# Moving the self term and the gate multiply of a selective scan out of the scan stage, with raw sums copied by ScalarE, a four-slot x^T ring, eight q slots and GpSimd multiplies in pairs

## The chip, the cores and the metric

One core of one Trainium2 chip runs the whole program in one launch. The metric is the time of the launch on the device in microseconds, lower is better. The profile has engines PE (TensorE; PEld is its weight load), DVE (VectorE), ACT (ScalarE), POOL (GpSimd) and SP (SyncE, which here only issues DMAs).

## What is computed

x has 2 x 4096 tokens of 512 columns. All arithmetic is fp32.

```python
xn = layernorm(layernorm(x)) * gamma + beta
x_ssm, z = split(xn @ W_in.T)                 # 1024 channels each
x_ssm = silu(causal_conv4(x_ssm) + conv_b)
xp = x_ssm @ W_xproj.T                        # 33 columns
B, C = xp[..., 1:17], xp[..., 17:33]
dt = softplus(xp @ W_dt.T + b_dt) + 0.001
# scan over time, 1024 channels x 16 states:
h = clip(exp(A*dt)*h + (1-exp(A*dt))/A * B * x_t, -10, 10)
y_t = sum_n(C_n * h_n) + D * x_t
x = x + (y * silu(z)) @ W_out.T
# mixture stage: shared product + one expert product scaled by the
# sum of the normalised top-2 gate weights
xf = layernorm(x)
out = x + xf @ W_shared.T + wsum * (xf @ W_expert.T) + bias
```

## The kernel before, in words

The program has four stages, one after another, each with its own block of instructions for every engine: `setup`, `front` (layer norm, input product, convolution, xp, dt; it writes x_ssm, silu(z), dt, a split transpose of x_ssm and B, C to DRAM), `scan`, and `ffn` (output product, residual, second layer norm, gates, shared and expert product). Every stage works on 16 chunks of 512 tokens. In `scan` a chunk has 8 blocks m of 128 channels, and a block has 16 steps, one for each state n. So there are 128 blocks and 2048 steps.

The scan keeps a transformed state. One step is spread over the engines:

- PE `make_d` (L896): a product of the transposed x (`xk`, two half-block slots) with a band matrix of B (`dm`, new for each chunk) gives one 512-column piece of d for the next block in one of two PSUM banks. ACT `move_d` (L847) copies it to `dd`.
- ACT `make_a` (L864): exp of dt times a constant, for the state three steps ahead, into one of four PSUM banks.
- DVE `states` (L1000): one scan instruction of 128x512 from `dd` and `ps_a` to one of 8 slots of `g`.
- POOL (L836): `q = g * C_n`, 128x512, in one of 4 slots of `q`. It waits for the scan and for the sum that frees the slot.
- PE `sum_state` (L917): a true fp32 product of q with a diagonal weight, added in `ps_y` over the 16 states, four steps (`LAG`) behind `make_d`.
- ACT `keep` (L871): every four steps, the last column of four g slots to `carry`.

Once a block there are four more operations. POOL multiplies B and C of the chunk (L815, once a chunk), PE weighs them (`weigh_bc`, L904, an fp32 product into a `ps_d` bank), DVE `self_term` (L961) makes `t = (ps_d + D) * x_ssm`, PE adds t to `ps_y` through the identity (L915), and DVE `finish` (L955) makes `y = ps_y * silu(z)` in the slot of z, which SP stores. DVE does `finish` after step 6 and `self_term` after step 7 of a block.

SP issues all loads of the scan from one queue in a written order with waits between them. For each block it loads dt, x_ssm, silu(z) (256 KB each), the diagonal weights (1.06 MB) and two halves of x^T (three pieces of 132 KB each). For each chunk it also loads `cc`, the spread C rows (four pieces of 1 MB), and `dm` (four pieces of three times 264 KB), both around the border between two chunks: `dm` in the block m = 6, `cc` in m = 7 and in m = 0 of the next chunk. Loads for the chunk after the last one wrap around to chunk 0, and so does the last block's `make_d`.

In `ffn`, PE does for each chunk 16 transposes (`L1241`), 96 matmuls of fp32r for the output product of the next chunk (four `project` calls), 12 for the gates, and 96 for the shared and expert products. fp32 operands are split in a high and a low part, with three matmuls for each pair of tiles. y is split by ACT (`y_hi`, L1167) and POOL (`y_lo`, L1145, 128x4096). POOL also adds the bias (L1159) and raises to the power -1/2 (L1140). The output product is made for one chunk ahead; in the last chunk it is made once more for chunk 0, and not used.

Of the kernel before, what the change touches and what calls it, by code (L numbers as in the profile page):

```python
# [4 lines left out]
P = 128  # L5
BATCH, LEN, DM = 2, 4096, 512
DI, NS, TAPS, NX = 1024, 16, 4, 33
TOKENS = BATCH * LEN
CH = 512
# [10 lines left out]
BLK = 32  # L20
# [23 lines left out]
def build(nc, t_in, out):  # L44
    with ExitStack() as ctx:
# [28 lines left out]
        scan(nc, sb, sem, ident, clips, xs_d, dt_d, zs_d, xp_d, xt_d, bt_d, band_d, c_d, w_d, y_d)  # L74
        ffn(nc, sb, sem, t_in, ident, minus_half, y_d, out)
# [524 lines left out]
def scan(nc, sb, sem, ident, clips, xs_d, dt_d, zs_d, xp_d, xt_d, bt_d, band_d, c_d, w_d, y_d):  # L600
    STEPS = MD * NS
    CHUNKS = BATCH * NCH
    AB, GB, QB = 4, 8, 4
    LEAD = 3
    LAG = 4
    HALF = NBLK // 2
    BC_AT, FINISH_AT, T_AT = 6, 6, 7
    PIECES = 4
    EACH = NBLK // PIECES
    with ExitStack() as c:  # L610
        w = sb("w_s", [P, 2, W_BIG], c=c)
        small = sb("small", [P, MD, W_SMALL], c=c)
        xs, dt = sb("xs_s", [P, 2, CH], c=c), sb("dt_s", [P, 2, CH], c=c)
        x_prev = sb("x_prev", [P, 2, 1], c=c)
        zs = sb("zs_s", [P, 2, CH], c=c)
        cc = sb("cc", [P, NS, CH], c=c)
        dm = sb("dm", [ROWS, NBLK, BLK, NS], F32R, c)
        xk = sb("xk", [ROWS, 2, HALF, P], F32R, c)
# [3 lines left out]
        t = sb("t", [P, CH], c=c)  # L622
        bc, c_r = sb("bc", [NS, CH], c=c), sb("c_r", [NS, CH], c=c)
        b_ahead = sb("b_ahead", [P, NS], c=c)

        neg_u0 = sb("neg_u0", [P, NS], c=c)
        fac, lim = sb("fac", [P, CH, 2], c=c), sb("lim", [P, CH, 2], c=c)
# [5 lines left out]
        s_pass, s_init = S("pass"), S("init")  # L633
        s_sm, s_band, s_bcl, s_ba = S("small"), S("band"), S("bcl"), S("ba")
        s_dm = [S(f"dm{i}") for i in range(PIECES)]
        s_xk, s_cc = [S("xk0"), S("xk1")], [S(f"cc{i}") for i in range(4)]
        s_dtl, s_wl, s_xsl, s_zsl = ([S(f"{n}{e}") for e in range(2)] for n in ("dt", "w", "xs", "zs"))
        s_bc, s_dps, s_dd, s_bcm, s_t = S("bc"), S("dps"), S("dd"), S("bcm"), S("t")
        s_a, s_g, s_q, s_n, s_fin = S("a"), S("g"), S("q"), S("n"), S("fin")
        s_car, s_zero, s_slow = S("carry"), S("zero"), S("slow")  # L640
        s_yo = [S("yo0"), S("yo1")]

        C_G, C_Q, C_N, C_FIN, C_T, C_CAR = AB, GB, LAG, 2, 1, 2

        def loads(ch, m):

            return ch * (16 * MD // 2) + 16 * (m // 2) + 16

        def scanned(ch, s):

            return ch * STEPS + s + C_G

        def multiplied(ch, s):

            return ch * STEPS + s + C_Q

        def summed(ch, s):

            return ch * STEPS + s + C_N

        with nc.Block() as block:
            @block.sync
            def _(sp):
                def load_x(b, k, m, h, n):
                    t0 = k * CH + (CH // 2) * h
                    for r, part in enumerate((0, 0, 1)):
                        src = xt_d[part, b, bass.ds(t0, BLK + 1), bass.ts(m, P)]
                        sp.dma_start(xk[(BLK + 1) * r:(BLK + 1) * (r + 1), h, :, :].bitcast(F32),
                                     bass.AP(tensor=src.tensor, offset=src.offset,
                                             ap=[(DI, BLK + 1), (BLK * DI, HALF), (1, P)])).then_inc(s_xk[h], 16)  # L670

                def fill_band(c, b, k):

                    for h in range(2):
                        sp.dma_start(band_d[c % 2, h, :, 0:2 * NS], bt_d[h, b, bass.ds(k * CH, CH + 1), :],
                                     allow_slow_non_contiguous=True).then_inc(s_band, 16)

                def load_b(c, i):
                    for r, part in enumerate((0, 1, 0)):
                        src = band_d[c % 2, part, bass.ds(BLK * EACH * i, BLK + 1), NS:2 * NS]  # L680
# [25 lines left out]
                def load_bc(b, k):  # L706
                    sp.dma_start(bc[:, :], xp_d[b, 1:1 + NS, bass.ds(k * CH + 1, CH)]).then_inc(s_bcl, 16)
# [668 lines left out]
```

## Time and profile before

| | us |
|---|---|
| median of 3 runs | 5179.3 (5155.68 to 5187.78) |
| the profiled execution's own time | 5171.58 |
| its span, first to last instruction | 5169.8 |
| scan, first to last DVE scan instruction | 1389.6 to about 4243 |
| first DMA of the last stage, its first matmul | 4259.66, 4285.25 |

| engine | busy share of the span |
|---|---|
| PE | 90% |
| DVE | 72% |
| ACT | 62% |
| POOL | 60% |

The shares are averages over stages with different limits. The granted TensorE clock is 0.94 of full speed in the mean. A busy time is a union of intervals: neighbouring instructions of an engine overlap by some tens of ns, so the spacing of instructions in a run of them is less than their mean duration.

### The profile page before, as it was taken

The page shows a single profiled execution, that of the slowest core. Times are in us where ns is not written, and L with a number is a line of the kernel's source. Part 1 is how long each engine was busy: PE and PEld are TensorE (multiplying, and loading weights), DVE is VectorE, ACT ScalarE, POOL GpSimd, SP SyncE. Part 2 cuts the span into 40 slices and gives each one's busy share as a digit, 9 for nine tenths or more (in the row PEclk, how much of TensorE's full clock was granted, in tenths as well). Part 3 has the DMA queues.
Part 4 walks back from the last instruction along what each step waited for, and adds up shares of the span by engine and source line. Part 5 has one row for each costly group of instructions (what it writes and reads, how often), then busy time and mean ns, then how long its engine had stood idle before and what let it go on. Part 6 is the DMA issues. An engine that isn't in the chain of part 4 may idle for free. (4 is left out here: it accounts for less than half of the span.)

```text
span 5169.8 us, 55997 instructions
## 1 busy us (share of the span) xinstructions
PE 4673.5 (90%) x14838; PEld 2749.7 (53%) x14838; DVE 3721.2 (72%) x4169; ACT 3205.7 (62%) x5723; POOL 3082.2 (60%) x2296
## 2 busy tenths in 40 slices
PE   4999999999598899989999989998899987999999
PEld 3566666666244444444444444444444446777777
DVE  5566666666498899889889988998898883333332
ACT  2545545545487788778888877887788772212111
POOL 1112122122298899889888988998898883322322
PEclk9889889889799999999999999999999998999999
DMA  4444444444656665665566566656655653222221
GB/s 176 145 153 163 158 150 164 161 146 165 190 163 177 190 171 170 181 190 169 170 185 185 163 179 182 174 163 191 182 172 165 191 170 130 81 81 81 81 72 66
DMA packets 590424, 807.29 MB, mean 156 GB/s; under 512 B 129738, under 2 KB 334866, under 8 KB 563735
## 3 DMA queue, kind: packets, MB, share of 16 engines
q1 hardware_dynamic: 544919, 721.30, 47.2%
q10 hardware_dynamic: 45312, 83.90, 4.3%
q8 instruction: 61, 1.00, 0.1%
q14 instruction: 132, 1.08, 0.1%
HBM read 561.72 MB, written 245.57 MB: 156 GB/s over the span
## 5 line engine op out<-in xcount | busy, mean ns | idle before, releaser
L836 POOL TENSOR_TENSOR q<-g,cc 128x512 f32<-128x512 f32 x2048 | 2535.9, 1277 | 329.8 <-PE ps_y L917 256.1
L1000 DVE TENSOR_TENSOR_SCAN g<-dd,carry,ps_a 128x512 f32<-128x512 f32 x2048 | 2444.4, 1257 | 256.6 <-ACT ps_a L864 140.7
L917 PE MATMUL ps_y<-q,w_s 128*128 128x512 f32 x4104 | 2186.6, 614 | 32.1 <-POOL q L836 32.1
L896 PE MATMUL ps_d<-dm,xk 99*128 99x512 f32 x2064 | 1650.9, 801 | 196.5 <-DMA xk<-xt_d 130.9
L847 ACT ACTIVATE dd<-ps_d 128x512 f32<-128x512 f32 x2064 | 1250.0, 606 | 550.2 <-PE ps_d L896 547.8
L864 ACT ACTIVATE ps_a<-dt_s,small 128x512 f32<-128x512 f32 x2051 | 1450.3, 707 | 0.0
L917 PEld LDWEIGHTS ps_y<-q,w_s 128*128 128x128 f32 x4104 | 794.0, 197 | 699.6 <-issue 405.2
L896 PEld LDWEIGHTS ps_d<-dm,xk 99*128 99x128 f32 x2064 | 403.3, 196 | 796.5 <-issue 653.4
L303 POOL TENSOR_TENSOR xnt_lo<-xnt_f,xnt_hi 128x512 fp32r<-128x512 f32 x68 | 92.3, 1359 | 622.0 <-ACT xnt_hi L329 619.6
L435 PE MATMUL ps_r_f<-xnt_hi,w_hi 128*128 128x512 f32 x1024 | 411.1, 401 | 12.1 <-ACT xz L345 7.5
L435 PE MATMUL ps_r_f<-xnt_hi,w_lo 128*128 128x512 f32 x1024 | 406.7, 397 | 0.0
L435 PE MATMUL ps_r_f<-xnt_lo,w_hi 128*128 128x512 f32 x1024 | 405.9, 396 | 0.0
L549 DVE SCALAR_TENSOR_TENSOR conv<-xz,taps,conv 128x512 f32<-128x512 f32 x384 | 352.0, 917 | 13.6
L1140 POOL TENSOR_TENSOR rstd_c<-var_c,minus_half 128x4 f32<-128x4 f32 x17 | 17.3, 1018 | 511.6 <-DVE var_c L1291 511.6
L315 POOL TENSOR_TENSOR lg_f<-lg_f,v_f 128x2048 f32<-128x2048 f32 x32 | 149.2, 4683 | 220.9 <-ACT lg_f L383 220.9
L1212 PE MATMUL ps_c<-wo_hi,y_hi 128*128 128x512 f32 x544 | 222.5, 409 | 40.4 <-DVE wo_lo L1299 37.8
L1283 DVE TENSOR_TENSOR x_c<-ps_c,x_c 128x512 f32<-128x512 f32 x68 | 47.0, 692 | 291.5 <-PE ps_c L1212 291.5
L435 PEld LDWEIGHTS ps_r_f<-xnt_hi,w_hi 128*128 128x128 f32 x1024 | 197.6, 193 | 58.4 <-ACT xz L345 11.1
L435 PEld LDWEIGHTS ps_r_f<-xnt_lo,w_hi 128*128 128x128 f32 x1024 | 197.2, 193 | 42.4
L435 PEld LDWEIGHTS ps_r_f<-xnt_hi,w_lo 128*128 128x128 f32 x1024 | 198.0, 193 | 40.5
L1212 PE MATMUL ps_c<-wo_lo,y_hi 128*128 128x512 f32 x544 | 218.5, 402 | 0.0
L1212 PE MATMUL ps_c<-wo_hi,y_lo 128*128 128x512 f32 x544 | 217.7, 400 | 0.0
(155 smaller groups left out, 4685.5 us busy)
## 6 DMA issues: line engine op xcount, KB each, us to landing
w_s<-w_d SPq DMA_DIRECT2D x129, 1088.0 KB, 5.1
xk<-xt_d SPq DMA_DIRECT2D x777, 132.0 KB
cc<-c_d SPq DMA_DIRECT2D x66, 1024.0 KB, 14.4
xt_d<-xt_f SPq DMA_DIRECT2D x256, 256.0 KB, 2.3
dm<-band_d SPq DMA_DIRECT2D x204, 264.0 KB
y_lo<-y_d SPq DMA_DIRECT2D x18, 2048.0 KB, 9.2
dt_s<-dt_d SPq DMA_DIRECT2D x129, 256.0 KB, 4.3
xs_s<-xs_d SPq DMA_DIRECT2D x129, 256.0 KB, 3.7
```

What stands on the lines that cost most here:

```text
L303: pool.tensor_tensor(xnt_lo[:, q, :], xnt[:, q, :], xnt_hi[:, q, :].bitcast(F32), ALU.subtract)\
L315: pool.tensor_tensor(lg[:, m0:m1, :], lg[:, m0:m1, :], v[:, m0:m1, :], ALU.add)\
L435: last = pe.matmul(ps_r[:, r % RING, :], wp[:, q, cols], xp_[:, q, :], start=(q + j == 0), stop=(q == KD - 1 and j == 2))
L549: dve.scalar_tensor_tensor(acc, xz[:, m, j:j + CH], taps[:, m, j:j + 1], acc, ALU.mult, ALU.add).then_inc(s_cv, 1)
L836: pool.tensor_tensor(q[:, s % QB, :], g[:, s % GB, :], cc[:, n, :], ALU.mult).then_inc(s_q, 1)
L847: act.activation(dd[:, m % 2, :, BLK * i:BLK * i + BLK], ps_d[:, ring(i), :].rearrange("p (t n) -> p n t", n=NS) if m == 0 else ps_d[:, (m ...
L864: act.activation(ps_a[:, s % AB, :], dt[:, m % 2, :], ACT.Exp, scale=small[:, m % MD, S_A + n:S_A + n + 1]).then_inc(s_a, 1)
L896: pe.matmul(ps_d[:, parity, :], xk[:, i // HALF, i % HALF, :], dm[:, i, :, :].rearrange("p t n -> p (t n)"), start=True, stop=True).then_i ...
L917: pe.matmul(ps_y[:, m % 2, :], w[:, m % 2, n * P:(n + 1) * P], q[:, s % QB, :], start=(n == 0), stop=(n == NS - 1)).then_inc(s_n, 1)
L1000: dve.tensor_tensor_scan(g[:, s % GB, :], dd[:, m % 2, n, :], ps_a[:, s % AB, :], carry[:, m, n:n + 1], ALU.add, ALU.mult).then_inc(s_g, 1)
L1212: last = pe.matmul(dst, a(j), b(j), start=(j + p == 0), stop=(j == tiles - 1 and p == 2))
L1283: dve.tensor_tensor(x[:, e, i, :], ps[:, i, :], x[:, e, i, :], ALU.add).then_inc(s_x1, 1)
```

## The change

In the scan stage the self term, the z load, the final multiply on DVE and its x_ssm load are gone. ACT copies the raw sum to a buffer `y` after step 10 of a block (`finish`), and that is what SP stores. POOL multiplies two steps at a time over 8 q slots, and the sums run six steps behind `make_d` instead of four. The x^T ring has four half-block slots, loaded up to a block further ahead. The pieces 2 and 3 of `cc` are issued at the end of m = 7 and the start of m = 0, and nothing is loaded or made past the last chunk. A path for clipping (not taken with these inputs) works in halves, to make room in SBUF.

In `ffn` the self term, the addition and the multiply by silu(z) are written out for every block of every chunk, for two chunks ahead. PE gets eight `weigh` products (48 rows, fp32r) per chunk, DVE eight `self_term` instructions, POOL sixteen 128x512 instructions (`mix`) and three for B * C (`weigh_rows`), SP eight loads each of x_ssm (ring of four) and silu(z) (ring of two). For chunk 0 DVE does the `mix`. `y_lo` is made in four parts. One half of a `project` is put between the second and the third transpose group, and the output product past the last chunk is left out. The weights are loaded from ACT's queue.

```diff
 def scan(...):
-    AB, GB, QB = 4, 8, 4
+    AB, GB, QB = 4, 8, 8
-    LAG = 4
+    LAG = 6
+    XB = 4
+    FINISH_AT = 10
 # SP
-                            load_x(*at(m + 1), 1, 0)
-                            load_dt_xs(*at(m + 1))
+                    load_x(blk + 2, 1)
+                    load_dt(blk + 1)
...
-                            load_x(*at(m + 2), 0, 0)
-                            load_zs(*at(m + 1))
+                    load_x(blk + 3, 0)
...
+                    if m == MD - 1 and more:
+                        sp.wait_ge(s_q, multiplied(NS * blk + 12))
+                        load_c(ch + 1, 2)
 # POOL
-                        pool.wait_ge(s_g, scanned(ch, s + 1))
-                        pool.wait_ge(s_n, summed(ch, s - QB + 1))
-                        pool.tensor_tensor(q[:, s % QB, :], g[:, s % GB, :], cc[:, n, :], ALU.mult).then_inc(s_q, 1)
+                    pool.wait_ge(s_g, s + 2)
+                    if s >= QB:
+                        pool.wait_ge(s_n, s - QB + 2)
+                    pool.tensor_tensor(q[:, s % QB:s % QB + 2, :], g[:, s % GB:s % GB + 2, :], cc[:, n:n + 2, :],
+                                       ALU.mult).then_inc(s_q, 2)
 # ACT
+                def finish(blk):
+                    act.wait_ge(s_n, NS * (blk + 1))
+                    if blk >= 2:
+                        act.wait_ge(s_yo[blk % 2], 16 * (blk // 2))
+                    act.activation(y[:, blk % 2, :], ps_y[:, blk % 2, :], ACT.Copy).then_inc(s_fin, 1)
 # PE: weigh_bc and the product with ident gone
 # DVE: finish and self_term gone
 def ffn(...):
 # SP, ring of two z tiles
+                def load_zs(ch, m):
+                        if piece(ch, m) >= ZRING:
+                            sp.wait_ge(s_mul, piece(ch, m) - ZRING + 1)
 # POOL, in each chunk
-                        rest_of_y(ch + 2, e, it * 16 + 32)
+                    mix(ch + 2)
+                    inverse_spread(ch + 1)
+                    rest_of_y(ch + 2)
+                    weigh_rows(ch + 3)
+                def mix(ch):
+                        for m in range(MD):
+                            pool.wait_ge(s_tt, piece(ch, m) + 1)
+                            pool.tensor_tensor(y[:, m, :], y[:, m, :], xs[:, m % XRING, :], ALU.add).then_inc(s_add, 1)
+                            pool.wait_ge(s_zsl[m % ZRING], 16 * (ch * (MD // ZRING) + m // ZRING + 1))
+                            pool.tensor_tensor(y[:, m, :], y[:, m, :], zs[:, m % ZRING, :], ALU.mult).then_inc(s_mul, 1)
 # DVE
+                def self_term(ch, m):
+                        dve.scalar_tensor_tensor(xs[:, m % XRING, :], ps_b[:, :], d_par[:, m:m + 1], xs[:, m % XRING, :],
+                                                 ALU.add, ALU.mult).then_inc(s_tt, 1)
 # PE, in each chunk
+                    turn(ch, 0)
+                    turn(ch, 1)
+                    project(ch + 1, 0, 0)
+                    turn(ch, 2)
+                    turn(ch, 3)
+                    weigh(ch + 2, 0)
+                    project(ch + 1, 0, 1)
```

## Rows read from the trace of the kernel before

**Rows 1.** Busy time by engine in two stretches: the scan, the last stage.

```profile
core 0: us, PE busy (x) PEld busy (x) DVE busy (x) ACT busy (x) POOL busy (x), PEclk, DMA share, GB/s
1399.00:4243.00 2844.00, 2633.64 (x6655) 1265.64 (x6654) 2582.39 (x2302) 2335.64 (x4605) 2552.50 (x2062) 0.96 0.62 177
...
4285.00:5170.00 885.00, 835.15 (x3680) 674.84 (x3680) 275.08 (x642) 160.37 (x181) 251.80 (x98) 0.97 0.23 78
```

**Rows 2.** Timeline of DVE in an undisturbed block (start, length, what).

```profile
2006.67 0.72 DVE L961 SCALAR_TENSOR_TENSOR t<-ps_d,small,xs_s 128x512 f32<-128x512 f32 x1
2007.32 17.67 DVE L1000 TENSOR_TENSOR_SCAN g<-dd,carry,ps_a 128x512 f32<-128x512 f32 x15
2024.90 0.66 DVE L955 TENSOR_TENSOR zs_s<-ps_y,zs_s 128x512 f32<-128x512 f32 x1
2025.49 1.27 DVE L1000 TENSOR_TENSOR_SCAN g<-dd,carry,ps_a 128x512 f32<-128x512 f32 x1
2026.67 0.72 DVE L961 SCALAR_TENSOR_TENSOR t<-ps_d,small,xs_s 128x512 f32<-128x512 f32 x1
```

**Rows 3.** Timeline of POOL, the undisturbed blocks of one chunk and one earlier run.

```profile
1999.03 9.87 POOL L836 TENSOR_TENSOR q<-g,cc 128x512 f32<-128x512 f32 x8
...
1966.95 121.92 POOL L836 TENSOR_TENSOR q<-g,cc 128x512 f32<-128x512 f32 x98 [0.80 <-PE ps_y L917]
```

**Rows 4.** Timeline of ACT and PE in undisturbed steps.

```profile
2003.07 0.59 ACT L847 ACTIVATE dd<-ps_d 128x512 f32<-128x512 f32 x1
2003.55 0.69 ACT L864 ACTIVATE ps_a<-dt_s,small 128x512 f32<-128x512 f32 x1
2004.16 0.20 ACT L871 ACTIVATE carry<-g 128x4 f32<-128x4 f32 x1
2004.26 0.59 ACT L847 ACTIVATE dd<-ps_d 128x512 f32<-128x512 f32 x1
...
2002.22 0.80 PE L896 MATMUL ps_d<-dm,xk 99*128 99x512 f32 x1
2003.31 0.80 PE L896 MATMUL ps_d<-dm,xk 99*128 99x512 f32 x1
```

**Rows 5.** Busy time, one whole chunk of the scan, and its border stretch.

```profile
1744.90:1922.60 177.70, 162.99 (x417) 78.43 (x416) 161.38 (x145) 145.93 (x290) 159.71 (x130) 0.97 0.63 178
1888.00:1966.00 78.00, 65.31 (x159) 30.84 (x158) 63.67 (x58) 56.12 (x110) 62.42 (x51) 0.93 0.84 218
```

**Rows 6.** Who waited for whom in the scan (total, times, longest).

```profile
PE ps_d L896 <- DMA xk<-xt_d: 120.8, 34, 6.6
DVE g L1000 <- ACT dd L847: 98.9, 45, 7.3
POOL q L836 <- DMA cc<-c_d: 61.9, 17, 5.8
```

**Rows 7.** Groups of POOL instructions of three widths (busy, mean ns).

```profile
L836 POOL TENSOR_TENSOR q<-g,cc 128x512 f32<-128x512 f32 x2048 | 2535.9, 1277 | 329.8 <-PE ps_y L917 256.1 <-DMA cc<-c_d 61.9 <-issue 0.5
L1145 POOL TENSOR_TENSOR y_lo<-y_lo,y_hi 128x4096 fp32r<-128x4096 f32 x18 | 162.8, 9044 | 20.8 <-ACT y_hi L1167 20.8
L315 POOL TENSOR_TENSOR lg_f<-lg_f,v_f 128x2048 f32<-128x2048 f32 x32 | 149.2, 4683 | 220.9 <-ACT lg_f L383 220.9
```

**Rows 8.** Last stage: chain by pieces, and PE's idle time at the transposes.

```profile
4378.17 11.72 PE ps_c L1212 x48
4389.89 2.80 PE ps_g L1212 x12
...
4799.67 12.54 PE ps_c L1212 x48
...
5135.89 28.10 PE ps_c L1212 x120
```

**Rows 9.** Timeline where the last stage starts.

```profile
4248.19 5.65 SPq L716 DMA_DIRECT2D y_d<-zs_s  x1
4259.66 0.38 SPq L1100 DMA_DIRECT2D o_c<-in_W_outT  x1
...
4267.05 2.29 DVE L1299 TENSOR_TENSOR wo_lo<-o_c,wo_hi 128x2048 fp32r<-128x2048 f32 x1 [18.89 <-ACT wo_hi L1171]
...
4274.19 8.85 POOL L1145 TENSOR_TENSOR y_lo<-y_lo,y_hi 128x4096 fp32r<-128x4096 f32 x1 [13.64 <-ACT y_hi L1167]
...
4275.95 9.25 DVE L1299 TENSOR_TENSOR wo_lo<-o_c,wo_hi 128x2048 fp32r<-128x2048 f32 x1 [6.60 <-ACT wo_hi L1171]
```

**Rows 10.** Timeline of PE in the last stage, with its idle time.

```profile
4641.15 1.09 PE L1241 MATMUL ps_t_c<-ident,xn_c 128*128 128x128 f32 x8 [2.51 <-DVE t_lo L1310]
```

**Rows 11.** DMA issues (count, KB each, us to landing).

```profile
zs_s<-zs_d SPq DMA_DIRECT2D x129, 256.0 KB, 3.8
bc<-xp_d SPq DMA_DIRECT2D x17, 32.0 KB, 14.6
```

More of the change, by code:

```diff
@@ L873, in _ @@
                 for i in range(NBLK):
[L874 removed]
+                    move_d(0, i)
                 act.wait_ge(s_sm, 16)
                 for s in range(LEAD):
[L877 to L886 removed]
+                    make_a(s)
@@ new lines, in rest_of_y @@
+                def rest_of_y(ch):
+                    if ch < CHUNKS:
+                        pool.wait_ge(s_yh, ch + 1)
+                        for j in range(YL):
+                            part = slice(2 * j, 2 * j + 2)
+                            pool.tensor_tensor(y_lo[:, part, :], y[:, part, :], y_hi[:, part, :].bitcast(F32), ALU.subtract)\
+                                .then_inc(s_yl, 1)
+                pool.memset(gate[:, :, :], -1.0).then_inc(s_set, 1)
+                pool.memset(raw_g, 0.0).then_inc(s_set, 1)
@@ new lines, in upper_y, with normalize @@
+                def upper_y(ch):
+                    if ch < CHUNKS:
+                        act.wait_ge(s_mul, piece(ch + 1, 0))
+                        if ch > 0:
+                            act.wait_ge(s_o, ch * SUB)
+                        act.activation(y_hi[:, :, :], y[:, :, :], ACT.Copy).then_inc(s_yh, 1)
+                def normalize(ch):
+                    if ch < CHUNKS:
+                        act.wait_ge(s_sh, ch + 1)
+                        for i in range(SUB):
+                            act.activation(xn[:, i, :], x[:, ch % 2, i, :], ACT.Identity, scale=rstd[:, i:i + 1],
+                                           bias=shift[:, i:i + 1]).then_inc(s_xn, 1)
@@ new lines, in store @@
+                def store(ch):
+                    act.wait_ge(s_fin, ch * SUB + SUB)
+                    act.dma_start(rows(out, ch), o[:, ch % 2, :, :]).then_inc(s_out[ch % 2], 16)
+                load_weights(1, "W_outT", 0)
+                load_weights(2, "W_outT", HALF * P)
+                load_weights(3, "W_sharedT", 0)
+                load_weights(4, "W_expertT", 0)
+                for i in range(3):
+                    upper_weights(i)
+                upper_y(0)
+                for i in range(3, len(parts)):
+                    upper_weights(i)
@@ L1220, in turn_gates @@
                     last.then_inc(s_g, 1)
-                def project(e, i):
-                    at = slice(i * P, (i + 1) * P)
-                    product(ps[:, i, :], lambda m: y_hi[:, m, at], lambda m: y_lo[:, e, m, at],
-                            lambda m: wo_hi[:, m, :], lambda m: wo_lo[:, m, :], MD).then_inc(s_o, 1)
-                pe.wait_ge(s_lo, 2)
-                pe.wait_ge(s_yl, 1)
+                pe.wait_ge(s_lo, 1)
+                for m in range(MD):
+                    weigh(0, m)
@@ L1270, in _, with step @@
                 at = [0]
-                def step(ins, base, wait=True):
+                def step(ins, wait=True):
                     at[0] += 1
```

951 lines of the change are left out of this document (481 added, 470 removed).

## The prediction

> **What bounds the kernel now.** I read busy time by stretch first, because the page's shares mix stages. In the scan's 2844 us DVE, PE and POOL are each busy for 90 to 93% of the time; in the last stage PE is for 94% and nothing else for over a third [rows 1]. So the scan is near a joint limit and the last stage is PE's. The front isn't touched.
>
> Next the timelines of an undisturbed block. DVE has no gap in it: 15 scans take 2024.90 - 2007.32 = 17.58 us, 1.172 each, one scan more takes 1.18, the self term holds DVE for 0.65 (2006.67 to 2007.32) and the final multiply for 0.59. Block after block that is 20.00 us (2006.67 to 2026.67) [rows 2]. POOL is as full: eight multiplies in a run begin 1.228 apart ((9.87 - 1.28) / 7), and 98 of them go without a gap worth a row [rows 3]. ACT needs 0.48 for a copy and 0.61 for an exp, 1.09 a step, and 0.10 more for a carry; PE's step is 1.09 too [rows 4].
>
> Last the borders. A chunk takes 177.7 us where eight blocks would be 160.0, so 17.7 us are lost per chunk [rows 5]. In the 78 us around a border DMA moves 218 GB/s with a busy share of 0.84, against 178 GB/s for the chunk, and the waits name the culprits: PE for `xk` 120.8 us in 34 waits, POOL for `cc` 61.9 in 17, DVE for `dd`, which is PE's stall handed on [rows 5, 6].
>
> **The change part by part.** The sum is made against the profiled execution's own 5171.6 us, 8 us under the median.
>
> *Undisturbed block.* DVE loses 0.65 + 0.59: 20.00 - 1.24 = 18.76 us. POOL would stay at 16 x 1.228 = 19.65 with single multiplies, so the pair's price decides. No row has a width of 1024. Between 1277 ns (512) and 4683 ns (2048) the line gives 1277 + 3406/3 = 2412 ns, towards 9044 ns (4096) it gives 2387 [rows 7]; less the 0.05 by which neighbours overlap, a pair holds POOL for 2.34 to 2.36 us, 18.7 to 18.9 a block. ACT has 16 x 1.09 + 4 x 0.10 and the new copy, 0.48 to 0.6: 18.4. PE has 16 x 1.09 = 17.4 [rows 4]. The largest is POOL's, so I take 18.9. Bounds are 18.76 (DVE alone) and 19.65 (a pair costs two singles). Gain: 128 x 1.1 = **141 us**, bounds 45 and 159. The wait for two scans puts POOL one step later; `LAG` 6 and eight q slots give the two steps back on the side of the sum, and g has eight slots, so I cost it at nothing. If that cover were gone each pair would wait for a PE step, which is the fourth rival's kind of loss.
>
> *Borders.* The two-slot x^T ring asks for a half within half a block, some 10 us, just when SP's queue is full. With four slots the load goes out a block or more ahead, past the 7.3 us of the longest wait. The last two `cc` pieces are asked for as soon as their slots are free, and per block 0.5 MB of x_ssm and silu(z) and 64 KB of weights are no longer loaded: 2.9 to 2.35 MB. Against a full cure: `dm` (3.2 MB) and `cc` (4.2 MB) still fall into about 52 us, with 2.75 x 2.35 = 6.5 MB beside them, 13.9 MB. At the 218 GB/s of [rows 5] that is 64 us, so a backlog of some 12 us builds up. `cc` and `dm` pieces have 12 to 15 us between slot free and use, and x^T over 20. So most is covered, not all. I take 5 us left of 17.7, bounds 0 and 17.7. Gain: 16 x 12.7 = **203 us**, bounds 0 and 283.
>
> *Ends of the scan.* The last store's issue waits 5.65 us in a queue full of loads for a chunk that isn't there, and 11.5 us pass until the next stage's first DMA [rows 9]. Those loads go: **-7**, bounds 0 and -10.
>
> *Start of the last stage.* First matmul 25.6 us after the first DMA now. The new chain: B and C rows land, three POOL instructions (3.8), `weigh`, then for eight blocks on DVE self term 0.7 and two operations of about 0.7 each. Silu(z) sits in a ring of two with a landing of 3.8 us [rows 11], issued behind the x, gate and bias loads, so I have the last block mixed at 38 us; `y_hi` 3.6 and `y_lo` 9.1 after it make 51. For chunk 1 POOL mixes before it serves the layer norm of chunk 0: another 4. **+31**, bounds +10 and +60.
>
> *PE's loop.* Eight `weigh` at the 2.80 / 12 = 0.233 us of a matmul [rows 8] are 1.9 us a chunk; the half `project` between the transposes covers the 2.5 us that PE waits there for `t_lo` [rows 10]. **-0.6 x 15 = -9**, bounds -20 and +30 with imperfect cover. DVE (five and a half us more) and POOL (below) have room beside 52.7 us a chunk, (4799.67 - 4378.17) / 8 [rows 8].
>
> *Last chunk.* 96 matmuls of a product that nobody reads are left out, 22.4 us on PE's path; 3 us of waits come out from under it. **-19**, bounds -15 and -22.
>
> Sum: -141 - 203 - 7 + 31 - 9 - 19 = **-348**, 5171.6 - 348 = 4824 us.
>
> One rule is weighed against a row. While POOL made `y_lo` from 4274.19 to 4283.04, a DVE subtract that takes 2.29 us took 9.25 and ended 2.2 us after POOL [rows 9]. The change puts POOL's `mix` beside three DVE instructions a chunk with both inputs in SBUF (the gate scaling, `pick`, `shift`). I count them at nothing, since PE has the 22 us of the shared and expert products to do and needs DVE's first sum only 11 us into them. The Trainium skill (SBUF — State Buffer, Who interferes with whom) says that a VectorE instruction with two SBUF inputs and a GpSimd instruction that reads SBUF block each other for a whole instruction; by that rule, the trace agrees. It also says that one with at most one SBUF input doesn't, which fits the scans running at full rate beside POOL [rows 2, 3]; what it would cost is the third rival.
>
> **The rivals.** (1) *The borders stay.* DMA volume, not ring depth, is the limit, and 12 us or more of the 17.7 remain. For: 218 GB/s and the backlog above. Against: most waits are for `xk` [rows 6]. Price at 16 us left: 16 x 11 = +176, 5000 us.
> (2) *A pair costs two singles.* POOL then sets 19.65 us a block: 128 x 0.75 = +96, 4920 us. That is also the case in which the change doesn't do what it says; the wide rows speak against it [rows 7].
> (3) *`mix` on POOL delays the gates* by a POOL instruction of 1.28 us for each of three or four DVE instructions, and the cover isn't there: 16 x 5 = +80, 4905 us.
> (4) *Slower than before.* POOL's loop in the last stage is 4 x 1.29 + 16 x 1.23 + 1.0 + 9.1 + 3.8 = 38.8 us. Silu(z) has two slots, so three turns of the ring take 3 x (landing + 1.6) in place of 3 x 4.9. With 3.8 us of landing nothing is lost. But small loads in a full queue landed after 14.6 us [rows 11]: the loop is then 72.7 us and the gain is down to 28. From 15.4 us on the whole gain is gone; at 18 us it is 83 us, 16 x 30 = +480, 5305 us. Against: DMA in the last stage carries 78 GB/s now [rows 1] and 4 MB more per chunk make it some 156, under the scan's 178 [rows 5].
> (5) *Nothing is left at the borders*: -80, 4745 us.
>
> **How the numbers follow.** Chances: forecast 0.50, (1) 0.13, (2) 0.12, (3) 0.08, (4) 0.05, (5) 0.12. The range 4730 to 4960 takes in the forecast with its bounds for the start, (2), (3) and (5); (1) and (4) lie above it. A change of 1% is about what a measurement of this kernel can tell. Faster by over 1%: 0.94; within 1%: 0.02 (the mild form of (4)); slower: 0.04.
>
> **What the changed profile would show.** Undisturbed blocks of 18.9 us with POOL gapless and DVE with small gaps; POOL pairs of about 2.41 us; hardly any wait of PE for `xk`; chunks of about 156 us. In the last stage chunks of about 52 us, no 2.5 us gap at the transposes, first matmul some 50 us after its first DMA. Wrong would be: pairs of 2.5 us, DVE or PE waiting over 10 us at each border, or PE in the last stage waiting for POOL's power or for `y_lo`.

## The result and the profile after

The changed kernel takes 4989.4 us (median of 4 runs, 4966.86 to 5004.33), 0.963 of the time before (95% interval 0.957 to 0.968). The forecast was 4825 with a range of 4730 to 4960: the sign was right, the size was not, 3.7% gained against 6.8%. The profiled execution took 4966.86 us. I cut it where the kernel does, at the first and last scan instruction and the first DMA of the last stage:

| stretch | before | after | change | forecast |
|---|---|---|---|---|
| start to first scan | 1389.6 | 1381.0 | -9 | 0 |
| first to last scan | 2852.3 | 2611.5 | -241 | -344 |
| last scan to first DMA of last stage | 17.7 | 7.6 | -10 | -7 |
| last stage | 910.1 | 965.0 | +55 | +3 |

The first line is scatter: other kernels with this front unchanged start their scan between 1366 and 1407 us. Almost the whole miss lies in the two large lines.

DVE's timeline over one chunk of the scan (start, length, what, idle before and its releaser), with the first and the last scans of all:

```profile
1380.98 3.62 DVE L927 TENSOR_TENSOR_SCAN g<-dd,carry,ps_a 128x512 f32<-128x512 f32 x3 [20.17 <-ACT ps_a L811]
...
1577.84 18.93 DVE L927 TENSOR_TENSOR_SCAN g<-dd,carry,ps_a 128x512 f32<-128x512 f32 x16 [10.84 <-ACT dd L800]
1598.22 131.30 DVE L927 TENSOR_TENSOR_SCAN g<-dd,carry,ps_a 128x512 f32<-128x512 f32 x112 [1.45 <-ACT dd L800]
1741.36 58.81 DVE L927 TENSOR_TENSOR_SCAN g<-dd,carry,ps_a 128x512 f32<-128x512 f32 x50 [11.83 <-ACT dd L800]
...
3899.84 92.62 DVE L927 TENSOR_TENSOR_SCAN g<-dd,carry,ps_a 128x512 f32<-128x512 f32 x79
```

Away from the borders DVE has no gap: 131.30 / 7 = 18.757 us a block, where it was 20.00 [rows 2]. At the border it still has gaps of 10.84 and 1.45 us. The chunk takes 1741.36 - 1577.84 = 163.5 us against 8 x 18.76 = 150.1, so 13.5 us are lost where 17.7 were [rows 5].

Over the whole scan that splits without a choice of chunk. I call what exceeds 128 undisturbed blocks the rest (borders and both ends): before 2852.3 - 128 x 20.00 = 292, after 2611.5 - 128 x 18.757 = 211. So blocks gave 159 us and the rest 82. The table of the experiments uses the same rest.

POOL in its longest run, with the page's group for it:

```profile
1600.81 112.47 POOL L789 TENSOR_TENSOR q<-g,cc 128x1024 f32<-128x1024 f32 x48 [1.53 <-DVE g L927]
```
```profile
L789 POOL TENSOR_TENSOR q<-g,cc 128x1024 f32<-128x1024 f32 x1024 | 2398.5, 2365 | 252.6 <-DVE g L927 93.8
```

A pair occupies POOL for 112.47 / 48 = 2.343 us, 18.75 a block, the lower end of the forecast's 2.34 to 2.36.

Who waited in the scan (total, times, longest):

```profile
DVE g L927 <- ACT dd L800: 189.3, 26, 15.2
ACT ps_a L811 <- DMA dt_s<-dt_d: 156.2, 16, 13.6
...
POOL q L789 <- DMA cc<-c_d: 39.6, 13, 4.2
```

PE no longer waits for `xk` at the borders (120.8 us in all in [rows 6]; one wait of 5.1 us is left, at the start). ACT waits for `dt_s` instead, once per border, 13.6 us at most where `xk` had 6.6. SP's own timeline at that border says why:

```profile
1703.94 5.98 SPq L691 DMA_DIRECT2D cc<-c_d  x1
1709.96 0.65 SPq L698 DMA_DIRECT2D b_ahead<-xp_d  x1
1710.66 10.43 SPq L700 DMA_DIRECT2D x_prev<-xs_d  x1
1721.13 1.75 SPq L706 DMA_DIRECT2D y_d<-y  x1
1722.92 0.55 SPq L691 DMA_DIRECT2D cc<-c_d  x1
1723.52 1.85 SPq L660 DMA_DIRECT2D xk<-xt_d  x3
1725.41 0.54 SPq L691 DMA_DIRECT2D cc<-c_d  x1
1725.99 0.59 SPq L683 DMA_DIRECT2D dt_s<-dt_d  x1
```

A 4 KB DMA keeps SP for 10.43 us. `dt_s`, due for the next block, is issued at 1725.99 behind it and behind two 1 MB pieces of `cc`, and ACT goes on at 1738.93 after 10.47 us of waiting. The load that is held stands directly behind `b_ahead`, 16 values of B for each of 128 partitions, 2048 single elements of 4 bytes in 8 KB. The same was so in the kernel before, where the three `xk` loads behind it held SP for 9.12 us:

```profile
1925.45 0.44 SPq L712 DMA_DIRECT2D b_ahead<-xp_d  x1
1925.93 9.12 SPq L668 DMA_DIRECT2D xk<-xt_d  x3
```

The last stage, in the chain that ended last (start, length):

```profile
4006.61 17.34 DMA y_c<-y_d
...
4048.13 14.34 POOL y_lo L1143 x4
4062.60 8.28 PE ps_c L1235 x24
...
4110.62 9.27 POOL y_lo L1143 x4
4119.93 5.49 PE ps_c L1235 x12
...
4151.30 24.79 PE ps_c L1235 x108
...
4205.30 24.79 PE ps_c L1235 x108
```

The first matmul of the output product comes 4062.6 - 4000.1 = 62.5 us after the stage's first DMA (25.6 before, [rows 9] and the table of times): +37. (The `weigh` products come before it, from 4017.59.) The product of chunk 1 starts 57.3 us later (37.4 before): +20. A chunk takes 54.0 us against 52.7 [rows 8]: 15 x 1.3 = +20. The unread product is gone: -21. Sum +56, of the +55 seen.

### The profile page after: what moved, and what is told of

Read it like the earlier page. It is cut to its first block and busy times, and to the rows that moved or that the text cites. A ratio compares the mean times of both kernels' runs of the same rounds, so it can differ in the third digit from the quotient of the medians.

```text
span 4965.1 us, 51915 instructions
## 1 busy us (share of the span) xinstructions
PE 4489.3 (90%) x14330; PEld 2559.1 (52%) x14330; DVE 3653.8 (74%) x4044; ACT 3221.7 (65%) x5827; POOL 3270.8 (66%) x1585
## 5 line engine op out<-in xcount | busy, mean ns | idle before, releaser
L927 DVE TENSOR_TENSOR_SCAN g<-dd,carry,ps_a 128x512 f32<-128x512 f32 x2048 | 2407.4, 1255 | 223.8 <-ACT dd L800 189.3
L789 POOL TENSOR_TENSOR q<-g,cc 128x1024 f32<-128x1024 f32 x1024 | 2398.5, 2365 | 252.6 <-DVE g L927 93.8
L867 PE MATMUL ps_y<-q,w_s 128*128 128x512 f32 x4096 | 2161.8, 609 | 122.0 <-POOL q L789 122.0
L811 ACT ACTIVATE ps_a<-dt_s,small 128x512 f32<-128x512 f32 x2048 | 1512.6, 739 | 161.6 <-DMA dt_s<-dt_d 156.2
L800 ACT ACTIVATE dd<-ps_d 128x512 f32<-128x512 f32 x2048 | 1299.1, 635 | 110.7 <-PE ps_d L856 94.5
L856 PE MATMUL ps_d<-dm,xk 99*128 99x512 f32 x2048 | 1205.6, 590 | 106.6 <-ACT dd L800 66.5
L435 PE MATMUL ps_r_f<-xnt_hi,w_hi 128*128 128x512 f32 x1024 | 410.4, 401 | 13.4 <-ACT xz L345 9.0
L549 DVE SCALAR_TENSOR_TENSOR conv<-xz,taps,conv 128x512 f32<-128x512 f32 x384 | 352.1, 917 | 13.6
L1132 POOL TENSOR_TENSOR y_c<-y_c,xs_c 128x512 f32<-128x512 f32 x120 | 154.5, 1288 | 164.2 <-DVE xs_c L1353 164.2
L504 DVE TENSOR_TENSOR xt_f<-ps_t_f,xt_f 128x512 fp32r<-128x512 f32 x128 | 88.1, 688 | 176.2 <-ACT xt_f L324 176.2
L1235 PE MATMUL ps_c<-wo_hi,y_lo 128*128 128x512 f32 x512 | 205.7, 402 | 0.0
L1235 PE MATMUL ps_c<-wo_lo,y_hi 128*128 128x512 f32 x512 | 205.1, 401 | 0.0
## 6 DMA issues: line engine op xcount, KB each, us to landing
cc<-c_d SPq DMA_DIRECT2D x64, 1024.0 KB, 14.9
```

Of the source, the lines that this page charges most:

```text
L435: last = pe.matmul(ps_r[:, r % RING, :], wp[:, q, cols], xp_[:, q, :], start=(q + j == 0), stop=(q == KD - 1 and j == 2))
L549: dve.scalar_tensor_tensor(acc, xz[:, m, j:j + CH], taps[:, m, j:j + 1], acc, ALU.mult, ALU.add).then_inc(s_cv, 1)
L789: pool.tensor_tensor(q[:, s % QB:s % QB + 2, :], g[:, s % GB:s % GB + 2, :], cc[:, n:n + 2, :], ALU.mult).then_inc(s_q, 2)
L800: act.activation(dd[:, blk % 2, :, BLK * i:BLK * i + BLK], ps_d[:, i % 2, :].rearrange("p (t n) -> p n t", n=NS), ACT.Copy).then_inc(s_dd, 1)
L811: act.activation(ps_a[:, s % AB, :], dt[:, blk % 2, :], ACT.Exp, scale=small[:, blk % MD, S_A + n:S_A + n + 1]).then_inc(s_a, 1)
L856: pe.matmul(ps_d[:, i % 2, :], xk[:, (2 * blk + i // HALF) % XB, i % HALF, :], dm[:, i, :, :].rearrange("p t n -> p (t n)"), start=True, s ...
```

## The experiments

All times are medians; "rest" is the scan's span in the run's one profiled execution less 128 x 18.757 us, "C landing" the median time from issue to landing of a `cc` piece. The runs were made in five groups (e1 to e4, e5 to e8, e9 to e12, e13 to e16, e17 and e18), and the kernel before had medians of 5169.4 to 5189.2 us beside them. So between groups 20 us of a median mean little, and the ratios and rests are the better measure.

| run | us | ratio to before (95%) | rest | C landing |
|---|---|---|---|---|
| after | 4989.4 | 0.963 (0.957 to 0.968) | 211 | 14.9 |
| e1_prev_spread | 4994.8 | 0.962 (0.956 to 0.967) | 220 | 15.8 |
| e2_dt_first | 4959.5 | 0.957 (0.952 to 0.962) | 189 | 14.8 |
| e3_no_cc_reload | 4797.2 | 0.926 (0.921 to 0.931) | 15 | not reloaded |
| e4_single_multiply | 5014.7 | 0.970 (0.963 to 0.977) | 234 | 13.2 |
| e5_two_xk_slots | 5009.2 | 0.967 (0.958 to 0.975) | 227 | 12.9 |
| e6_no_dm_reload | 4893.5 | 0.943 (0.935 to 0.950) | 122 | 10.4 |
| e7_weigh_128_rows | 4946.9 | 0.953 (0.945 to 0.961) | 214 | 14.9 |
| e8_weigh_twice | 4995.2 | 0.964 (0.957 to 0.972) | 213 | 15.0 |
| e9_cc_ring_of_five | 4906.8 | 0.949 (0.945 to 0.954) | 129 | 15.1 |
| e10_cc_from_distinct_rows | 4865.4 | 0.943 (0.938 to 0.947) | 95 | 10.3 |
| e11_before_no_cc_reload | 4984.0 | 0.966 (0.962 to 0.971) | 92* | not reloaded |
| e12_ring_pad_early | 4864.8 | 0.942 (0.938 to 0.946) | 125 | 14.3 |
| e13_copies_32 | 4869.5 | 0.938 (0.933 to 0.942) | 100 | 10.4 |
| e14_copies_128 | 5144.1 | 0.991 (0.988 to 0.994) | 102 | 11.3 |
| e15_best_128_copies | 5051.4 | 0.974 (0.969 to 0.979) | 53 | 10.3 |
| e16_no_ring_128_copies | 5072.7 | 0.978 (0.973 to 0.983) | 73 | 10.2 |
| e17_best_32_copies | 4760.7 | 0.919 (0.916 to 0.922) | 51 | 10.5 |
| e18_no_ring_32_copies | 4782.8 | 0.921 (0.917 to 0.925) | 69 | 10.2 |

\* against 128 x 20.00, the blocks of before, whose own rest is 292.

**e1: `x_prev` in eight small DMAs, one per block.** Is the held SP the fault of that DMA's 4-byte pieces?

```diff
-                    sp.dma_start(x_prev[:, :], xs_d[b, :, :, bass.ds(k * CH, 1)].rearrange("m p o -> p (m o)"), ...)
+                    if m > 0 and more:
+                        load_prev(ch + 1, m - 1)        # 128 elements each
```

> The changed kernel with x_prev (1024 elements of 4 bytes, one DMA at the chunk border) loaded in eight DMAs of 128 elements, one in each block. Theory A (that DMA holds SP's queue for 10 us at the border, so that dt for the next block goes out late): the wait of ACT for dt falls from 156 us in all to under 50, a border costs 13.5 - 10 = 3 to 5 us, the time falls by 16 x 9 = about 145, to 4845. Theory B (the volume of dm and cc at the border is the limit): SP is held by the next DMA instead, a border keeps over 10 us, the time falls by less than 40.

No gain. SP at the same place of the border:

```profile
1735.90 0.99 SPq L698 DMA_DIRECT2D b_ahead<-xp_d  x1
1736.93 10.09 SPq L703 DMA_DIRECT2D x_prev<-xs_d  x1
```

An eighth of the pieces is held for as long, while the median of all 128 small loads is 0.43 us: the time isn't the load's own, and the name in the row is that of a victim. What stands in front of it is the same at all 15 borders: `b_ahead`. The load behind it is held for 10.1 to 12.0 us here, 10.4 to 11.9 in the kernel after, 8.2 to 9.6 (three `xk` loads) in the kernel before, 6.5 to 8.3 in e13, where C is read faster, and 4.6 to 7.7 in e3, where it isn't reloaded; elsewhere in the scan of the kernel after, its start and end aside, no load or store holds SP for over 7 us. So C has a part in it, and `b_ahead`'s single elements may have another. Only the path for clipping uses `b_ahead` and `x_prev`, so they could have been left out; no run does that.

**e2: dt ahead of a chunk's last `cc` piece in SP's order.** `x_prev` stays ahead of both.

```diff
                     load_x(blk + 2, 1)
+                    sp.wait_ge(s_a, NS * blk + 1)
+                    load_dt(blk + 1)
                     if m == 0:
...
                         load_c(ch, 3)
-                    sp.wait_ge(s_a, NS * blk + 1)
-                    load_dt(blk + 1)
```

> The changed kernel with the load of dt in a chunk's first block put ahead of the last cc piece. Theory A: x_prev's DMA still holds SP ahead of both, dt gains one cc piece of transfer at most, 16 x 4 = 64 us or less. Theory B: dt jumps one of the queued megabytes, 4 us a border, 64 us. Theory C (only the written order of dt behind cc is at fault): the wait for dt goes, 16 x 9 = 145 us.

The median falls by 30 us, the rest by 22, half of the 64 that theories A and B allow and far from theory C's 145. ACT's wait is down, and others grow in its place:

```profile
PE ps_y L867 <- POOL q L789: 155.0, 65, 12.8
DVE g L927 <- ACT dd L800: 139.5, 29, 15.2
ACT dd L800 <- PE ps_d L856: 99.2, 71, 9.3
ACT ps_a L811 <- DMA dt_s<-dt_d: 90.2, 19, 8.3
```

The order decides who is late, not whether somebody is.

**e3: C is loaded for the first chunk only. e6: the same for `dm`.**

```diff
                 def load_c(ch, i):
+                    if ch > 0:
+                        return
```

All later chunks then multiply by the first chunk's C, or in e6 use its B.

> The changed kernel with cc loaded for the first chunk alone, so that all later chunks multiply by the first chunk's C (that part of the computation is changed). 4.2 MB less at each border, x_prev's DMA kept. Theory B: the border's loss goes, 16 x 13 = about 200 us. Theory A: the DMA of small pieces still takes as long to issue, but dt no longer queues behind 2 MB; half of the loss may stay, 60 to 110 us gained.

> The changed kernel with dm (the band of B) loaded for the first chunk alone, so that later chunks use the first chunk's B (that part of the computation is changed). 3.2 MB less at each border, cc kept. Volume theory: the deficit of 2.8 MB (12 us at 218 GB/s) goes: -150 to -200 us, as without cc. If it is something of the cc loads themselves (their slow packets, or POOL's wait on them): less than -80 us.

Without the reload of C 192 us go, and with them the borders. The busy times of 1200 us in the middle of that scan (length, PE, PEld, DVE, ACT, POOL, clock, DMA share, GB/s):

```profile
2000.00:3200.00 1200.00, 1185.23 (x3072) 516.00 (x3071) 1199.34 (x1025) 1184.32 (x2368) 1199.10 (x512) 1.00 0.50 150
```

DVE misses 0.7 us of 1200. Without the reload of `dm` 96 us go, between the two expectations. Both are far more than the waits for these loads: `cc` has 39.6 us there, `dm` 4.3. The sum of bytes doesn't hold in full either: without `dm`'s 3.2 MB the backlog of the prediction's sum (12 us at 218 GB/s, 2.6 MB) would be gone, and still over half of the rest stays (122 of 211).

**e4: one step per multiply. e5: two x^T slots.** The two parts of the change that the forecast valued most, each undone.

```diff
-                for s in range(0, BLOCKS * NS, 2):      # e4
+                for s in range(BLOCKS * NS):
...
-    XB = 4                                              # e5, loads one block later
+    XB = 2
```

> The changed kernel with POOL multiplying one step at a time, still with eight q slots and the sums six steps behind. If POOL's time per step sets the block, blocks go from 18.75 to 19.65 us, +115 us less what the borders' waits absorb, 80 to 115. If DVE's scan sets it with room to spare on POOL, no change.

> The changed kernel with two half-block slots for x^T, as before the change, each loaded when its slot is free. Volume theory (what a border loses is DMA bytes over rate; the depth of the x^T ring matters little): 0 to +25 us. Depth theory of the prediction (most of the border's loss in the kernel before was the two-slot ring): +100 us or more, with PE waiting for xk as before, 100 us or more in all.

Pairs are worth 25 us, where 80 to 115 were expected, four slots 20; each is at the edge of what the intervals resolve. POOL in e4:

```profile
2068.40 152.72 POOL L789 TENSOR_TENSOR q<-g,cc 128x512 f32<-128x512 f32 x124 [2.00 <-DMA cc<-c_d]
```

Singles take 152.72 / 124 = 1.232 us, 157.7 for a chunk's 128. The borders make a chunk last 164 anyway, and DVE's blocks beside it still take 18.8 us: POOL falls behind inside the buffers and catches up at the border. While borders cost 13 us, a dearer multiply hides in them. In e5 PE waits 187.4 us for `xk`, more than before the change, and it costs 20.

**e7: `weigh` on 128 rows, the lower 80 zero. e8: each 48-row `weigh` twice.**

```diff
-        inv = sb("inv_c", [ROWS3, MD, P], F32R, c)
+        inv = sb("inv_c", [P, MD, P], F32R, c)        # e7, b_r alike
...
+                        pe.matmul(ps_b[:, :], inv[:, m, :], b_r[:, :], start=True, stop=True)   # e8
                         pe.matmul(ps_b[:, :], inv[:, m, :], b_r[:, :], start=True, stop=True).then_inc(s_bcm, 1)
```

> The changed kernel with the operands of weigh padded with zeros from 48 to 128 rows. In the trace a weigh adds 0.63 us to PE, 0.40 more than a matmul of 128 rows. If the change of row count between neighbouring matmuls costs that: 112 weighs in the loop x 0.40 = -45 us. If it comes from the change of weights, operands or PSUM bank: no change.

> The changed kernel with every weigh product done twice in a row. If the switch into and out of 48 rows costs, the second one costs a plain 0.23 us: +30 us. If each matmul of 48 rows costs 0.63: +75 us.

A `weigh` among its neighbours in the kernel after, then in e8 (start, busy time of one):

```profile
4305.30 0.40 PE L1235 MATMUL ps_c<-wo_hi,y_lo 128*128 128x512 f32 x1
4305.63 0.50 PE L1245 MATMUL ps_b<-b_r,inv_c 48*128 48x512 f32 x1
4306.06 0.50 PE L1235 MATMUL ps_c<-wo_hi,y_hi 128*128 128x512 f32 x1
4306.39 0.39 PE L1235 MATMUL ps_c<-wo_lo,y_hi 128*128 128x512 f32 x1
```
```profile
4302.54 0.39 PE L1235 MATMUL ps_g<-t_hi,wg_lo 128*128 128x512 f32 x1
4302.86 0.49 PE L1245 MATMUL ps_b<-b_r,inv_c 48*128 48x512 f32 x1
4303.19 0.39 PE L1246 MATMUL ps_b<-b_r,inv_c 48*128 48x512 f32 x1
4303.52 0.50 PE L1235 MATMUL ps_c<-wo_hi,y_hi 128*128 128x512 f32 x1
4303.85 0.39 PE L1235 MATMUL ps_c<-wo_lo,y_hi 128*128 128x512 f32 x1
```

From 4305.30 to 4306.39 three steps take 1.09 us; two matmuls of 128 rows would take 0.46, so the `weigh` adds 0.63. With two of them it is 4302.54 to 4303.85, 1.31 us, so the second adds 0.22 or 0.23 and a 48-row matmul itself costs what a wide one does (the loop grows from 54.0 to 55.8 us, 8 x 0.23; the median, 6 us up, doesn't resolve that). The other 0.40 is the change of row count, there and back. On 128 rows it is gone:

```profile
4172.57 24.59 PE ps_c L1239 x108
4223.64 24.58 PE ps_c L1239 x108
```

The spacing over the loop is 51.05 us per chunk, 15 x 2.95 = 44 us less; the median says 42.

**e9: a ring of five C pieces, with dt first.** If C is the cost, a piece asked for four blocks ahead should hide it. SBUF for the fifth comes from three x^T slots and six q slots.

```diff
-        cc = sb("cc", [P, NS, CH], c=c)
+        cc = sb("cc", [P, NS + 4, CH], c=c)
...
+                    at = 4 * ((4 * ch + i) % 5)
...
+                    if m == 3 and more:
+                        sp.wait_ge(s_q, multiplied(NS * MD * ch))
+                        load_c(ch + 1, 0)
```

> The changed kernel with a ring of five cc pieces, so that one of the four megabytes per chunk is loaded in the quiet block m = 3; to make room q has six slots (sums five steps behind) and x^T three, and dt is loaded ahead of cc as in the run with dt first. Volume theory: 1.05 MB less at a border is 5 us at 218 GB/s, 75 us over 15 borders beyond the 30 of dt first: about -105 against the changed kernel, if the smaller rings cost nothing. If order or ring depth rules: the smaller rings cost more than this gives, 0 or slower.

-83 us where 105 were expected, 53 of it beyond e2 (60 by the rest). The other three pieces still fall at the border.

**e10: as many bytes to `cc`, but each partition reads a row of its own (of dt).** In the kernel C lies in 16 copies, and eight partitions read each.

```diff
-                    src = c_d[:, ch // NCH, ch % NCH, 4 * i * CH:(4 * i + 4) * CH]
+                    src = dt_d[ch // NCH, (ch + i) % MD, :, (i % 2) * 4 * CH:(i % 2) * 4 * CH + 4 * CH]
```

> The changed kernel with cc loaded with the same bytes, packets of 8 KB and places in the queue, but from rows of dt that are distinct for each partition (that part of the computation is changed), where the kernel reads each row of C for eight partitions. cc's packets take 550 ns for 8 KB, those of w 392 to 467 for 8.7 KB. If reading one row eight times is what makes them slow: packets of 400 to 450 ns, the border's loss falls by a third to a half, -60 to -100 us. If the bytes alone count: no change.

124 us less by the medians, 116 by the rest, at the same volume, and a piece lands in 10.3 us, not 14.9. So at one volume it matters much how the rows are read; e6 shows that the volume counts too.

**e11: the kernel before, C loaded once.** Was that so already?

> The kernel before with cc loaded for the first chunk alone. Volume theory: its 17.7 us a border was mostly queueing behind bytes too, so nearly all goes, -200 to -270 us. Depth theory of the prediction (the two-slot x^T ring is the cause): PE still waits for xk, less than half goes, under -130 us.

Yes: the time falls by 185 us (5169.4 for the kernel before beside it), the rest from 292 to 92. So 200 us of the old borders hung on C, where the waits had 61.9 for `cc` and 120.8 for `xk` [rows 6].

**e12: e9, e7 and the weight parts split ahead of the first `mix`.**

```diff
-                for i in range(3):
+                for i in range(5):
                     upper_weights(i)
                 upper_y(0)
```

> The ring of five cc pieces with dt first, weigh padded to 128 rows, and the low parts of the weights made on DVE before the first chunk's mix, where DVE waits for y (in the changed kernel they share time with POOL's y_lo, which takes 14.3 us there in place of 9.3). Sum of the parts: -105 - 42 - 6, to about 4835.

-42 against e9, which e7 explains alone; the sum of the parts, 4835, is missed by 30 us. The early weights do what they should, but it is little: `y_lo` takes 9.69 us at the start and ends 65.5 us after the last scan, not 14.34 and 70.0.

**e13 and e14: 32 and 128 copies of C, so four partitions and one read a row.** e10 changed the place of the rows too; these change only the sharing (and the size of the front's store of C), and compute the right thing.

```diff
-COPIES = 16
+COPIES = 32     # e14: 128
```

> The kernel after with 32 copies of C in DRAM in place of 16, so that each row of C is read by four partitions in place of eight. The scan's loads keep their number and size; the front writes 0.5 MB more per chunk. Theory A (reads of one row by many partitions are slow, and that is most of what the distinct rows gained: -124 us): a part of that gain comes with each halving; with two halvings left after this one I expect 30 to 60 us less than the kernel after, 4930 to 4960, and cc landing after 12 to 14 us. Theory B (not the sharing; the distinct rows gained because they came from other places of DRAM, or because their bytes were just read by others): no change, 4980 to 5000, landing 14.9.

> The kernel after with 128 copies of C, one for each partition: no row is read twice, as with the distinct rows, but the product is the right one. The front writes 3.5 MB more per chunk in a store of its own, at 218 GB/s some 16 us of DMA beside 80 us of work; the front has DMA to spare, so 0 to +10 us in all, if the store doesn't delay the next ones in its queue. Theory A: scan span falls by about 130 to 150 us as with the distinct rows (4865), landing about 10.3 us, in all 4860 to 4900. Theory B: scan unchanged, 4990 to 5020 in all. If the front pays more than 50 us for the store, theory A can be right in the scan and the total still 4920.

One number makes the kernel 120 us faster. Both have about the rest of e10 (100 and 102, with 95 there) with C's own tensor, so sharing is the cause and the place of dt's rows isn't. I expected the gain to come in steps and the time with 32 copies to be 4930 to 4960; all of it comes between eight readers and four. The 36 us up to the first scan behind a border, in the kernel after, in e13 and in e6 (columns as above):

```profile
1705.00:1741.00 36.00, 25.54 (x61) 10.94 (x60) 24.53 (x21) 23.67 (x48) 24.68 (x12) 0.89 0.91 207
```
```profile
1710.00:1746.00 36.00, 30.34 (x74) 13.20 (x73) 29.46 (x26) 28.46 (x58) 29.89 (x14) 0.92 0.86 255
```
```profile
1708.00:1744.00 36.00, 30.86 (x76) 13.13 (x75) 30.20 (x27) 29.40 (x60) 30.62 (x14) 0.95 0.92 216
```

The DMA engines are nearly as busy and move 255 GB/s, not 207. e6, with eight readers and no `dm`, still moves only 216 at a share of 0.92. Neighbouring borders say the same: 202 to 212 in the kernel after, 243 to 266 in e13. The landing is the weaker sign. It falls from 14.9 to 10.4 us in e13, but it is 10.4 in e6 with eight readers too, and 12.9 to 15.8 in the other runs with 16 copies: it counts what stands in the queue as well.

128 copies lose it all in the front, where I had allowed 10 us: its store is 4 MB per chunk and stands in SP's queue ahead of the others. The scan starts at 1669 us, not 1381, DVE waits there 410.4 us for `x_f` (67.7 in the kernel after), and the read of x lands after 11.7 us, not 6.5.

**e15 to e18: is the late C one cause or two?** e12's version and the same without the longer ring (dt first, `weigh` on 128 rows and early weights stay), with 128 and with 32 copies.

> The version with the five-piece ring of C, the 128-row weigh, the early weight parts and dt first (4864.8), with 128 copies of C. Theory A: packets and ring both shorten the same waits, so the gains don't add: borders of 8.7 us are left of which half goes, 40 to 90 us less, 4775 to 4825. Theory B: 4865 or more.

> As the last, but without the ring of five C pieces and with the four x^T slots and eight q slots of the kernel after. Theory A: the faster landing does by itself what the ring does; 4780 to 4840, within 30 us of the version with the ring. Theory B: no gain from copies, so only the parts -30 (dt first), -42 (weigh) and some -20 (early weights) remain: 4900.

> The version with the five-piece ring of C, the 128-row weigh, the early weight parts and dt first (4864.8), with 32 copies of C, which cost the front nothing that the run with 32 copies shows apart (its scan started at 1405 us, that of other runs with an unchanged front between 1366 and 1407). With 128 copies the scan of this version fell by some 60 us against 16 copies; theory A: 32 copies do the same, 4790 to 4820. Theory B (the ring already hides what the slow reads cost): within 15 us of 4865.

> The same without the ring of five C pieces, with four x^T slots and eight q slots as in the kernel after. Theory A (one cause, late C pieces, cured twice): 5 to 25 us more than with the ring, as with 128 copies (5072.7 against 5051.4): 4800 to 4840. Theory B (two causes): 40 us or more above the version with the ring.

With dt first the rest is 189 (e2). The ring alone makes it 125 to 129, the copies alone 69, both 51: the gains of 60 to 64 and 120 don't add to 180 or more but give 138. That is what one cause would do, C pieces that come late: a faster read cures most of it and a longer lead a part of what is left. e15 and e16 missed their numbers by e14's front (5144.1 - 4869.5 = 275 us); less that they lie at 4777 and 4798, inside them. e17 and e18 came out below theirs, and differ by 22 us, inside the 5 to 25 of one cause. e17 is the fastest kernel here, 4760.7 us, 0.919 of before. Its scan, and what waits are left:

```profile
2016.61 18.85 DVE L929 TENSOR_TENSOR_SCAN g<-dd,carry,ps_a 128x512 f32<-128x512 f32 x16 [2.93 <-ACT dd L802]
2035.64 131.31 DVE L929 TENSOR_TENSOR_SCAN g<-dd,carry,ps_a 128x512 f32<-128x512 f32 x112 [0.18 <-ACT dd L802]
2168.99 150.04 DVE L929 TENSOR_TENSOR_SCAN g<-dd,carry,ps_a 128x512 f32<-128x512 f32 x128 [2.03 <-ACT dd L802]
```
```profile
DVE g L929 <- ACT dd L802: 47.4, 25, 6.9
ACT ps_a L813 <- DMA dt_s<-dt_d: 44.5, 14, 5.9
```

A chunk is 2168.99 - 2016.61 = 152.4 us, 2.3 above eight blocks.

## Why the prediction was right or wrong

- **Undisturbed block: right.** 18.9 us forecast, 18.76 measured; 141 against 159 us. DVE and POOL are within 0.01 us of each other, so the line through other widths (2.34 to 2.36) sized the pair well. But the rival "a pair costs two singles", priced at +96, was priced without the borders' waits, in which a slower POOL catches up; with those that stayed, e4 cost 25.
- **Borders: the step that failed.** "So most is covered, not all. I take 5 us left of 17.7." 13.5 were left; the rest fell by 82 us, not by the 210 of border and end terms. Two things were wrong. The cause was read off the wait with the largest total, `xk`. e5 and e11 show that it wasn't: with two slots PE waits for `xk` again and 20 us are lost, and without C's reload 200 of 292 us go even in the old kernel. `xk` was the small load that stood behind `cc` and `b_ahead` in one queue; the change took it out of the way, and `dt_s` took its place. And the backlog of 12 us, which the step worked out itself, was let off against the "12 to 15 us between slot free and use" of single pieces. But the pieces share one queue with all that is due sooner, so a backlog of 12 us delays those too. Taken at its word that sum leaves 12 us a border, 4825 + 16 x 7 = 4937 us; 13.5 were measured. That nearness is in part luck: the sum makes bytes at one rate the whole of it, and e6 and e13 show that it isn't (without `dm` no backlog is left in the sum, but 1743.99 - 1587.96 - 8 x 18.757 = 6.0 us are lost at the border in e6's trace; with four readers the bytes are the same and 111 us of the rest go). The case stood as the first rival, with 16 us and 5000, at a chance of 0.13.
- **The first rival was right in size and half right in reason.** It blamed the volume. The same volume from rows with four readers costs 110 us less of scan (e13) and moves at 255 GB/s, so 207 GB/s was the rate of this way of reading. The forecast used [rows 5]'s 218 GB/s as if it were a property of the DMA. Less volume helps as well (96 us in e6).
- **Ends of the scan: right**, -7 against -10.
- **Start of the last stage: too small**, +31 against +57. The `mix` of chunk 0 was done 44.3 us after the first DMA, not 38. `y_lo` was set at 9.1 and took 14.33, since DVE's weight splits run beside it (in e12, where they come earlier, it takes 9.69):

```profile
4044.32 4.49 DVE L1339 TENSOR_TENSOR wo_lo<-o_c,wo_hi 128x2048 fp32r<-128x2048 f32 x2
4048.13 14.33 POOL L1143 TENSOR_TENSOR y_lo<-y_c,y_hi 128x1024 fp32r<-128x1024 f32 x4 [30.68 <-ACT y_hi L1184]
4049.88 3.28 DVE L1339 TENSOR_TENSOR ws_lo<-xn_c,ws_hi 128x2048 fp32r<-128x2048 f32 x1 [1.08 <-ACT ws_hi L1176]
4053.09 4.42 DVE L1339 TENSOR_TENSOR we_lo<-xb_c,we_hi 128x2048 fp32r<-128x2048 f32 x1
4057.43 2.82 DVE L1339 TENSOR_TENSOR wg_lo<-x_c,wg_hi 128x512 fp32r<-128x512 f32 x1
```

 The last takes 2.82 us for a quarter of the elements that take 3.28, so it is mostly waiting. By the rule of the Trainium skill (SBUF — State Buffer, Who interferes with whom) cited in the prediction such DVE and POOL instructions take turns; the trace agrees, 14.33 us beside them and 9.27 for the same four at 4110.62. The prediction applied it to the loop and not to the start, where it costs 5 us on the path. Chunk 1's `mix`, priced at 4, and its `weigh` products amid the first output products, cost 20 together.
- **PE's loop: wrong sign**, -9 against +20, by one price: `weigh` at the 0.233 us of a 128-row matmul, where it costs 0.63. e7 makes it 0.23, and the loop is 51.05 us, 1.6 under before; the cover of the transposes was, if anything, better than the 0.6 forecast.
- **Last chunk: right**, -19 against -21.
- **The other rivals.** `mix` does delay the gates (the gate scaling takes 1021 ns in the mean, 188 before; `pick` 452, 167 before), 1.1 us a chunk, and nothing waits for it. The ring of two z tiles never decides: a z tile lands after 3.0 us.

What stays open: why eight readers of a row are slow and four are not; what `b_ahead`'s single elements add at a border; and the 36 us between e17's rest and that of e3. Cures with fewer bytes (C spread on the chip, not by DMA) weren't tried.

## What to carry to other kernels

In one ordered queue the wait with the largest total names the load that is due first, not the one that fills the queue; leave one load out at a time before you price a cure. When a sum of bytes over rate exceeds the time there is, don't let the excess off against the slack of single loads; here it came near the delay (12 against 13.5 us), though not all of the delay was volume. A load that takes long to issue may be held by the one in front: look there first. Look at GB/s per busy share of the DMA: if it is low, change how rows are read before you change how much or when. An engine's excess over the bound is free only while the stall elsewhere lasts, so a part's worth measured now isn't its worth after the next cure.

## What the runs showed of the hardware

- Loads of 1 MB whose DRAM rows are read by eight partitions each keep the DMA slow: at the border 207 GB/s at a busy share of 0.91, with four readers 255 at 0.86, and 111 us of the scan's rest go. One reader gives no more (rests of 95 and 102 against 100). With all other loads the same such a piece lands after 14.9 us with eight readers and 10.4 with four; with less beside it (e6) one with eight readers lands in 10.4 too.
- Behind a load of 2048 single elements, in a queue with 1 MB loads from rows with eight readers, SP is held for 10 to 12 us at the DMA that comes next, even at one of 128 elements (10.09 us) that takes 0.43 in the median; with four readers the hold is 6.5 to 8.3 us (e13), without these loads 4.6 to 7.7 (e3).
- A 48-row fp32r matmul among 128-row ones adds 0.63 us where a 128-row one adds 0.23; two in a row share the extra 0.40. With zero rows up to 128 the extra is gone (e7).
